# Two attention layers and a mixture of experts on one core: norm pieces of the first attention moved, its first scores issued inside the projections, two ScalarE tables fetched ahead, one low part given to VectorE

## The chip, the cores and the metric

The kernel runs on one core of a Trainium2 chip. Its time is the device time of one execution in microseconds. Each run is compared by its median; a profile is one execution recorded by the hardware profiler, and all stretches below count from the start of its span.

## What is computed

```python
x = L0_attn_x                                   # (4, 512, 256) fp32
x = x + _layernorm(attn(_layernorm(x), Wq, Wk, Wv, Wo))       # 16 heads of 16, causal
x = x + _layernorm(ffn(_layernorm(x), ...))
# ffn(h):
#   r   = rmsnorm(h, ln1_w);  16 heads of 128, causal, scale 192 ** -0.5
#   hid = h + attention(r) @ o_w.T
#   x2  = rmsnorm(hid, ln2_w)
#   w   = top 4 of softmax(x2 @ gate_w.T), normalised to sum 1     (16 experts)
#   routed = sum_e w_e * (silu(x2 @ g_e.T) * (x2 @ u_e.T)) @ w2_e.T   (176 wide)
#   shared = (silu(x2 @ sg.T) * (x2 @ su.T)) @ sh_down_w.T            (352 wide)
#   return hid + routed + shared
```

All of it is fp32; matmuls split their operands into a high part (fp32r) and a low part, and add three products.

## The kernel before

The 2048 rows (4 batches of 512) stay in SBUF as 16 tiles of 128 rows. Each engine has one instruction stream written out in order, and the streams meet through semaphores. They run through six stages.

**Projections of the first attention** (0 to 55 us). For each batch `b`, TensorE turns the normalised rows (`turn_x`), multiplies them into four banks of q and k, then into two banks of v. ScalarE copies the high parts and v out of PSUM (`ph1_hi`, `ph1_v`), VectorE forms the low parts (`ph1_lo`). Banks 0 and 1 hold the turned rows, banks 2 to 5 q and k, banks 6 and 7 v.

**First attention** (55 to 243 us): 32 steps `step1(s)`, two heads of one batch each, 8 steps to a batch. SyncE builds a "stack" for each step out of the high and low parts of q and k: seven DMAs into one of `NSTK = 4` slots (`load_stack`, line 379 for six of them, line 381 for the last), followed by one DMA that clears scratch rows in HBM (line 385). The load of step `s + 4` waits until TensorE has finished the scores of step `s`. In a step:

- TensorE computes scores of the *next* step (line 1564: the widest three blocks `S1_PARTS` early, the rest `S1_REST` later), VectorE takes the row minima of the negated scores (line 1113), TensorE turns them (line 1527, `least`), ScalarE copies them into the stack (line 837, two small copies), TensorE computes the transposed scores with that row (line 1571), ScalarE takes five exponentials (line 832), GpSimd clears the future (line 520), TensorE multiplies with the values (line 1581).
- Every second step ScalarE copies the sums out (line 850, `o_sum`), TensorE turns them, VectorE weighs them (line 1174); every fourth step TensorE turns the output and ScalarE copies it (`take_oT`, line 856).
- One batch later its rows are projected, normed and added, a piece at a time, at steps counted by `k = s % 8` and `b = s // 8 - 1`: projection at `k == 2`, `scale_u` at `k == 5` (two tiles by ScalarE, line 804; two by VectorE), the sum `x1` by GpSimd after it, GpSimd's roots at `k` 3, 4, 6, 7, and `scale_xn` at `k == 0` (two tiles by ScalarE, line 810; two by VectorE, line 1136), which waits for GpSimd's `m_rms`. The normed rows are turned at `k == 4`.

What ScalarE does in its `step1` after the stack copies, in order, in the kernel before: exponentials 0 and 1, `o_sum`, `take_oT` at `s % 8 == 1`, `scale_xn` at `k == 0`, exponentials 2 to 4, `take_oT` at `s % 8 == 5`, `scale_u` at `k == 5`. VectorE has `scale_xn` between the two groups of minima.

All engines then meet at a fence. **Second attention** (248 to 945 us): 64 heads, one after the other. **Shared expert and routing of the last batch** (945 to 1021 us): 12 pieces `s`, each with an up product on TensorE, silu by ScalarE (line 990), the product with the other half by VectorE (line 1385), its high part by ScalarE (line 994), its low part `hh_lo` by GpSimd for `s < LO_POOL = 6` (line 729) and by VectorE for the rest (line 1395), and the down product, which waits for `hh_lo`. Between them stand the norm and the routing of the last batch: squares on ScalarE (line 897), roots of them on GpSimd (12 small instructions, ahead of its first `hh_lo`), the scaled rows (lines 1223 and 904), their transposes (line 1681), copies (line 909 and 1228), logits, ranks and places on VectorE, and the sending of rows by GpSimd. **Experts** (1021 to 1195 us): 79 tiles, loaded by SyncE once all rows are sent. **End**: sums, norm, store.

ScalarE's functions come in tables. The exp table is loaded where the first exponential stands, the silu table where the first silu stands (ACT_TABLE_LOAD in the trace).

Of the kernel before, what the change touches and what calls it, by code (L numbers as in the profile page):

```python
# [17 lines left out]
ACT = mybir.ActivationFunctionType  # L18
# [3 lines left out]
P = 128  # L22
# [9 lines left out]
def sandwich_kernel(nc, x_d, qkv1_d, wo1_d, qkvo2_d, ln_w_d, gate_d, moe_d, stack_d, out_d):  # L32
# [40 lines left out]
    with ctx:  # L73
# [399 lines left out]
        def _(pool):  # L473
# [258 lines left out]
            root_of_squares(B - 1)  # L732
            for s in range(LO_POOL):
                shared_lo(s)
# [12 lines left out]
        def _(act):  # L747
# [75 lines left out]
            free = bank[FREE_BANK]  # L823

            def step1(s):
                b, k = s // (N1 // B) - 1, s % (N1 // B)

                def exp(i):
                    act.wait_ge(a1_st, 6 * s + (i + 1 if i < 2 else i + 2))
                    if i == 0 and s >= 2:  # L830
                        act.wait_ge(a1_pv, s - 1)
                    act.activation(pT1[:, s % 2, i, :], st1(s, i)[:, :], ACT.Exp).then_inc(a1_exp, 1)  # L832

                if s < N1:
                    act.wait_ge(a1_mt, s + 1)
                    for a in range(2):
                        act.activation(stk[64 * a:64 * a + 1, s % NSTK, 0, :], st1(s, 0)[64 * a:64 * a + 1, :], ACT.Copy)\
                           .then_inc(a1_m, 1)
                if b >= 0 and k == 2:
                    take_y(b, 0, free)  # L840
                if b >= 1 and k == 4:
                    take_xT(b - 1, 0, free)
                if s < N1:
                    exp(0)
                    exp(1)
                if s >= 2 and s % 2 == 0:

                    act.wait_ge(a1_pv, s)
                    act.wait_ge(a1_ot, s // 2 - 1)
                    act.activation(o1_sum[:, :], bank[O1_BANK][:, :], ACT.Copy).then_inc(a1_oe, 1)  # L850
                def take_oT():
                    g = (s - 5) // 4
                    act.wait_ge(a1_xt, g + 1)
                    if g >= 2:
                        act.wait_ge(m_y, 2 * (g // 2))
                    act.activation(oT1[:, g % 2, :], free[:, :], ACT.Copy).then_inc(a1_o, 1)

                if s >= 5 and s % 8 == 1:
                    take_oT()
                if b >= 0 and k == 2:  # L860
                    take_y(b, 1, free)
                if b >= 1 and k == 0:
                    scale_xn(b - 1)
                if b >= 1 and k == 4:
                    take_xT(b - 1, 1, free)
                if s < N1:
                    for i in range(2, 5):
                        exp(i)
                if s % 8 == 5:
                    take_oT()  # L870
                if b >= 0 and k == 5:
                    scale_u(b)

            for s in range(N1 + 2):
                step1(s)
# [100 lines left out]
            for n in range(N2 + 2):  # L976
                step2(n)
            squares(B - 1)
            def w1_half(c, gu):
# [59 lines left out]
        def _(dve):  # L1039
# [115 lines left out]
            def step1(s):  # L1155
# [32 lines left out]
                if b >= 0 and k == 5:  # L1188
                    scale_u(b)
                if b >= 1 and k == 0:  # L1190
                    scale_xn(b - 1)
                if s + 1 < N1:
# [3 lines left out]
                if b >= 1 and k == 4:  # L1196
                    take_xT(b - 1, 1, free)
                if b >= 0 and s < N1 and k == 2:
                    y_stats(b)
# [179 lines left out]
            for s in range(SHARED + 1):  # L1379
# [6 lines left out]
                if s and s % SHR == 0:  # L1386
# [3 lines left out]
                    for i in range(2):  # L1390
                        two = hs[:, TPB * b + 2 * i:TPB * b + 2 * i + 2, :].rearrange("p j d -> p (j d)")
                        dve.tensor_tensor(two, two, bank[6 + i][:, :], ALU.add).then_inc(f_acc, 1)
                if LO_POOL <= s < SHARED:
                    dve.wait_ge(f_hh, s + 1)
                    dve.tensor_tensor(hh_lo[0:rows, s % 2, :], gated[0:rows, s % 2, :], f32(hh_hi[0:rows, s % 2, :]),
                                      ALU.subtract).then_inc(f_lod, 1)
# [77 lines left out]
        def _(pe):  # L1474
# [7 lines left out]
            def turn_x(b):  # L1482
# [3 lines left out]
                for c in range(C):  # L1486
# [3 lines left out]
                    ins.then_inc(ph1_tp, 1)  # L1490

            turn_x(0)
            for b in range(B):
# [8 lines left out]
                if b + 1 < B:  # L1502
                    turn_x(b + 1)
                if b == 0:
                    pe.wait_ge(ph1_wl, 2)
                else:
                    pe.wait_ge(ph1_v, b * 2)
# [45 lines left out]
            pe.wait_ge(ph1_lo, 4 * B)  # L1553
            pe.wait_ge(ph1_v, 2 * B)
            pe.wait_ge(a1_zero, 3)
            free = bank[FREE_BANK]

            def step1(s):
# [27 lines left out]
                r = s + 1  # L1586
                if r < N1:
                    pe.wait_ge(stk_in[r % NSTK], 16 * 7 * (r // NSTK + 1))
                    for i, (a, n) in enumerate(S1_PARTS):
                        if r >= 1:  # L1590
                            pe.wait_ge(a1_max, 6 * (r - 1) + i + 4)
                        score(r, a, n).then_inc(a1_s, 1)
# [226 lines left out]
            def shared_down(s):  # L1819
                b, r = s // SHR, s % SHR  # L1820
                rows = shared_rows(r)
                if s < LO_POOL:
                    pe.wait_ge(f_lop, s + 1)
                else:
                    pe.wait_ge(f_lod, s - LO_POOL + 1)
                if b and r == 0:
# [161 lines left out]
```

## Time and profile before

| what | value |
|---|---|
| median of 3 runs | 1240.77 us (1239.87 to 1243.07) |
| the profiled execution | 1242.91 us, its span 1241.2 us |
| TensorE busy in matmuls | 1178.2 us, 95% of the span |
| VectorE, ScalarE, GpSimd busy | 861.5, 794.0, 577.1 us |
| first attention, 80 to 100 us | TensorE 19.05 of 20 us, ScalarE 16.25, VectorE 16.75 |
| second attention, 500 to 600 us | TensorE 100.0 of 100 us |
| mean granted clock of TensorE | 0.986 of full speed |

The busy shares are averages over stages with different limits. The chain of waits follows the work that ended last back to what released it; the timeline gives each engine's instructions with their start, their time and, in brackets, how long the engine had been idle and what ended that.

### The profile page before, as it was taken

The page shows a single profiled execution, that of the slowest core. Times are in us where ns is not written, and L with a number is a line of the kernel's source. Part 1 is how long each engine was busy: PE and PEld are TensorE (multiplying, and loading weights), DVE is VectorE, ACT ScalarE, POOL GpSimd, SP SyncE. Part 2 cuts the span into 40 slices and gives each one's busy share as a digit, 9 for nine tenths or more (in the row PEclk, how much of TensorE's full clock was granted, in tenths as well). Part 3 has the DMA queues.
Part 4 walks back from the last instruction along what each step waited for, and adds up shares of the span by engine and source line. Part 5 has one row for each costly group of instructions (what it writes and reads, how often), then busy time and mean ns, then how long its engine had stood idle before and what let it go on. Part 6 is the DMA issues. An engine that isn't in the chain of part 4 may idle for free.

```text
span 1241.2 us, 25176 instructions
## 1 busy us (share of the span) xinstructions
PE 1178.2 (95%) x7996; PEld 1007.7 (81%) x7996; DVE 861.5 (69%) x2662; ACT 794.0 (64%) x1971; POOL 577.1 (47%) x845
## 2 busy tenths in 40 slices
PE   6899999889999999999999999999998889999986
PEld 5756555579999998999989999989997769999962
DVE  5677887677667666886667876777865855555535
ACT  3387777767768776677676777776776534444422
POOL 3053645545333444537443366433363346666650
PEclk9989999999999999999999999999999989999998
DMA  8955555175733112122212122121214247777766
GB/s 266 283 160 174 172 167 152 51 213 152 213 109 95 54 55 87 48 70 83 86 35 69 35 68 105 35 68 35 69 61 113 68 124 122 117 118 119 117 113 218
DMA packets 111780, 139.59 MB, mean 112 GB/s; under 512 B 11364, under 2 KB 94820, under 8 KB 111524
## 3 DMA queue, kind: packets, MB, share of 16 engines
q1 hardware_dynamic: 97204, 119.10, 31.6%
q0 software_dynamic: 14448, 18.88, 9.4%
q8 instruction: 69, 1.13, 0.4%
q14 instruction: 59, 0.48, 0.1%
HBM read 63.36 MB, written 61.87 MB: 101 GB/s over the span
## 4 chain that ended last, share of the span: by engine, by line
PE 70%; DVE 12%; ACT 8%; issue 4%; POOL 3%; DMA 2%; SPq 1%; POOLq 0%; ACTq 0%; DVEq 0%
PE bank L1478 49%; PE bank L1887 5%; PE bank L1710 5%; DVE bank L1113 3%; PE bank L1527 3%; PE bank L1581 2%; ACT p L953 2%; PE bank L1564 2%; DVE hs L1336 2%; ACT pT L832 2%; DVE pT L1323 1%; PE bank L1866 1%; PE bank L1897 1%; PE bank L1571 1%; DVE qk L1212 1%
## 5 line engine op out<-in xcount | busy, mean ns | idle before, releaser
L1113 DVE CUSTOM_DVE_ANT_0 bank<-bank,mask 128x512 f32<-128x512 f32 (+3 forms) x512 | 235.2, 523 | 35.8 <-PE bank L1564 23.1
L944 ACT ACTIVATE p<-bank,stat 128x512 f32<-128x512 f32 (+3 forms) x256 | 131.7, 528 | 132.2 <-DVE stat L1113 132.2
L533 POOL CAST w_hl<-raw_qkv 128x512 fp32r<-128x512 f32 x96 | 58.8, 613 | 312.3 <-DMA raw_qkv<-in_qkvo 162.6
L1478 PE MATMUL bank<-xT,w_hl 128*128 128x512 f32 x768 | 189.2, 395 | 0.0
L1478 PEld LDWEIGHTS bank<-xT,w_hl 128*128 128x128 f32 x768 | 144.1, 188 | 34.1
L742 POOL DMA_INDIRECT sum_rows<-mid,goal x79 | 122.9, 1555 | 70.7 <-DVE mid L1442 69.2
L1478 PE MATMUL bank<-pT,v 128*128 128x128 f32 (+3 forms) x768 | 137.1, 327 | 0.0
L953 ACT ACTIVATE p<-p,stat 128x512 f32<-128x512 f32 (+3 forms) x256 | 123.1, 553 | 14.7 <-DVE stat L1339 14.7
L1478 PE MATMUL bank<-qk 128*128 128x512 f32 (+3 forms) x768 | 129.4, 317 | 3.2 <-DVE pT L1323 2.4
L1478 PEld LDWEIGHTS bank<-qk 128*128 128x128 f32 x768 | 119.3, 189 | 12.1 <-DVE v L1212 2.6
L534 POOL TENSOR_TENSOR w_hl<-raw_qkv,w_hl 128x512 fp32r<-128x512 f32 x96 | 124.2, 1294 | 7.8
L1361 DVE TENSOR_TENSOR o<-bank,o 128x512 fp32r<-128x512 f32 x64 | 44.2, 690 | 109.4 <-ACT o L960 109.4
L1478 PEld LDWEIGHTS bank<-pT,v 128*128 128x128 f32 x768 | 109.7, 190 | 2.9
L1478 PE MATMUL bank<-wo_hl,o 128*128 128x256 f32 x768 | 107.2, 289 | 2.8 <-DVE o L1361 1.4
L1323 DVE TENSOR_TENSOR pT<-bank,pT 128x128 fp32r<-128x128 f32 (+3 forms) x256 | 107.2, 481 | 0.0
L1478 PEld LDWEIGHTS bank<-w_hl,xT 128*128 128x128 f32 x768 | 98.8, 188 | 9.5 <-issue 4.3
L1478 PE MATMUL bank<-w_hl,xT 128*128 128x256 f32 x768 | 101.5, 280 | 1.9 <-DVE xT L1228 1.9
L832 ACT ACTIVATE pT<-bank 128x512 f32<-128x512 f32 x160 | 85.2, 602 | 24.8 <-PE bank L1571 23.2
L1478 PEld LDWEIGHTS bank<-wo_hl,o 128*128 128x128 f32 x768 | 95.6, 190 | 4.3 <-issue 2.5
L1478 PE MATMUL bank<-w_hi,sh_hi 128*128 x316 | 97.2, 349 | 0.5 <-issue 0.4
L1212 DVE SCALAR_TENSOR_TENSOR qk<-bank,qk 128x512 fp32r<-128x512 f32 x128 | 82.4, 683 | 21.7 <-ACT qk L886 21.4
L936 ACT ACTIVATE pT<-bank 128x128 fp32r<-128x128 f32 (+3 forms) x256 | 91.1, 454 | 0.0
(232 smaller groups left out, 2404.0 us busy)
## 6 DMA issues: line engine op xcount, KB each, us to landing
raw_qkv<-in_qkvo SPq DMA_DIRECT2D x32, 768.0 KB, 5.7
xs_rows<-blank SPq DMA_DIRECT2D x32, 520.0 KB, 3.3
xs_rows<-blank SPq DMA_DIRECT2D x5, 2730.0 KB, 14.3
xrow<-xs_rows SPq DMA_DIRECT2D x79, 130.0 KB, 2.5
raw_o<-in_qkvo SPq DMA_DIRECT2D x32, 256.0 KB, 3.7
sum_rows<-blank SPq DMA_DIRECT2D x3, 2176.0 KB, 8.5
stk<-xT SPq DMA_DIRECT2D x96, 64.0 KB
stk<-k_hl SPq DMA_DIRECT2D x96, 64.0 KB
```

Of the source, the lines that this page charges most:

```text
L534: pool.tensor_tensor(lo, raw, f32(hi), ALU.subtract).then_inc(done, 1)
L742: pool.indirect_dma_start(sum_d[i % NSUM], bass.IndirectOffsetOnAxis(goal[:, i % NY:i % NY + 1], 0), yt[:, i % NY, :], None, compute_op=AL ...
L832: act.activation(pT1[:, s % 2, i, :], st1(s, i)[:, :], ACT.Exp).then_inc(a1_exp, 1)
L936: act.activation(pT2[:, HI, QOFF[kj]:QOFF[kj + 1]], bank[t][:, 0:TB - P * kj], ACT.Copy).then_inc(b_pth, 1)
L944: act.activation(p2[:, n % 2, POFF[qi]:POFF[qi + 1]], s2(t), ACT.Exp, scale=-1.0, bias=stat2[:, 0, n % 2, t:t + 1], accum_out=stat2[:, 1, ...
L953: act.activation(pt, pt, ACT.Copy, scale=stat2[:, 2, n % 2, t:t + 1]).then_inc(b_norm, 1)
L1113: return dve.tensor_tensor_reduce(scores, scores, mask[:, TB - scores.shape[1]:], scale=-1.0, scalar=-2.0 * MASKED, op0=ALU.add, op1=ALU.m ...
L1212: dve.scalar_tensor_tensor(lo, qkv_bank(n, i)[:, :], SCALE2 if i == 0 else 1.0, f32(hi), ALU.mult, ALU.subtract).then_inc(b_lo, 1)
L1323: dve.tensor_tensor(pT2[:, LO, QOFF[kj]:QOFF[kj + 1]], bank[t][:, 0:TB - P * kj], f32(pT2[:, HI, QOFF[kj]:QOFF[kj + 1]]), ALU.subtract).th ...
L1478: ins = pe.matmul(out, a, b, start=start and i == 0, stop=stop and i == len(pairs) - 1, **kw)
L1710: ins = pe.transpose(bank[t][:, P * (qi - kj):P * (qi - kj + 1)], p2[:, (n - 1) % 2, POFF[qi] + P * kj:POFF[qi] + P * (kj + 1)], ident[:, :])
L1887: ins = pe.matmul(bank[6 + i % 2][:, 0:D], ht[:, i % 2, P * h:P * (h + 1)], w2r[:, ds(expert[i], 1), h, :].rearrange("p a n -> p (a n)"), ...
```

## The change

1. The wait for all value copies (`ph1_v`, 8) goes from TensorE's start of the first attention, and the three widest score blocks of step 0 (`first_scores`) are issued in the last batch's projections, after q and k and ahead of v.
2. ScalarE's `take_oT` of `s % 8 == 5` stands in the next step, right after its stack copies.
3. ScalarE's `scale_u` stands between exponentials 1 and 2 of the same step, no longer at its end.
4. `scale_xn` of ScalarE and VectorE stands at the end of the step with `k == 1`, no longer in the middle of the one with `k == 0` (only for the last batch it stays at `k == 0`, after the last step).
5. A one-element exponential ahead of `step1(0)` and a one-element silu ahead of the last `squares` load the two tables there.
6. The low part of the first shared piece is VectorE's; GpSimd has pieces 1 to 5.

```diff
@@ gpsimd
-            for s in range(LO_POOL):
+            for s in range(1, LO_POOL):
                 shared_lo(s)
@@ scalar, step1
+                if s >= 6 and s % 8 == 6:
+                    take_oT((s - 6) // 4)
                 if b >= 0 and k == 2:
                     take_y(b, 0, free)
...
                     exp(0)
                     exp(1)
+                if b >= 0 and k == 5:
+                    scale_u(b)
                 if s >= 2 and s % 2 == 0:
...
                 if s >= 5 and s % 8 == 1:
-                    take_oT()
+                    take_oT((s - 5) // 4)
                 if b >= 0 and k == 2:
                     take_y(b, 1, free)
-                if b >= 1 and k == 0:
-                    scale_xn(b - 1)
...
                     for i in range(2, 5):
                         exp(i)
-                if s % 8 == 5:
-                    take_oT()
-                if b >= 0 and k == 5:
-                    scale_u(b)
-
+                if b >= 1 and k == (1 if s < N1 else 0):
+                    scale_xn(b - 1)
+
+            act.activation(sm[:, 10, 0:1], ident[:, 0:1], ACT.Exp)
             for s in range(N1 + 2):
                 step1(s)
...
             for n in range(N2 + 2):
                 step2(n)
+            act.activation(sm[:, 9, 0:1], ident[:, 0:1], ACT.Silu)
             squares(B - 1)
@@ vector
-                if b >= 1 and k == 0:
-                    scale_xn(b - 1)
...
+                if b >= 1 and k == (1 if s < N1 else 0):
+                    scale_xn(b - 1)
...
-                if LO_POOL <= s < SHARED:
+                if s == 0 or LO_POOL <= s < SHARED:
                     dve.wait_ge(f_hh, s + 1)
@@ tensor
+            def first_scores():
+                pe.wait_ge(stk_in[0], 16 * 7)
+                for a, n in S1_PARTS:
+                    if n == 2:
+                        pe.wait_ge(ph1_lo, 4 * (B - 1) + 1)
+                    rows = slice(64 * a, 64 * a + 64)
+                    pe.matmul(s1(a, n), stk[rows, 0, 0, P * (n - 1):P * n], stk[rows, 0, 1, 0:P * n],
+                              start=True, stop=True).then_inc(a1_s, 1)
...
                 if b + 1 < B:
                     turn_x(b + 1)
+                else:
+                    first_scores()
...
-            pe.wait_ge(ph1_v, 2 * B)
...
-                if s < LO_POOL:
-                    pe.wait_ge(f_lop, s + 1)
+                if 1 <= s < LO_POOL:
+                    pe.wait_ge(f_lop, s)
                 else:
-                    pe.wait_ge(f_lod, s - LO_POOL + 1)
+                    pe.wait_ge(f_lod, s - LO_POOL + 2 if s else 1)
```

The order of instructions at three places, before and now.

TensorE, end of the projections and step 0 of the first attention (`bank<-stk` are scores; the row of 24 with 128x256 is v of the last batch). Before:

```order
L1478 MATMUL bank<-xT,qkv_hl 128x512 x24
L1478 MATMUL bank<-qkv_hl,xT 128x256 x24
L1564 MATMUL bank<-stk 128x512 x2
L1564 MATMUL bank<-stk 128x256
L1564 MATMUL bank<-stk 128x384 x2
```

Now:

```order
L1479 MATMUL bank<-xT,qkv_hl 128x512 x24
L1500 MATMUL bank<-stk 128x512 x2
L1500 MATMUL bank<-stk 128x256
L1479 MATMUL bank<-qkv_hl,xT 128x256 x24
L1576 MATMUL bank<-stk 128x384 x2
```

Three score matmuls have moved ahead of the 24 of v.

ScalarE, steps 16 and 17 of the first attention (`stk<-bank` are the stack copies at the start of a step, `pT<-bank` exponentials, `xn_mid` is `scale_xn`). Before:

```order
L837 ACTIVATE stk<-bank 1x512 x2
L832 ACTIVATE pT<-bank 128x512 x2
L850 ACTIVATE o_sum<-bank 128x512
L810 ACTIVATE xn_mid<-x_sb,midst 128x256 x2
L832 ACTIVATE pT<-bank 128x512 x3
L837 ACTIVATE stk<-bank 1x512 x2
L832 ACTIVATE pT<-bank 128x512 x2
L856 ACTIVATE oT<-bank 128x512
L832 ACTIVATE pT<-bank 128x512 x3
L837 ACTIVATE stk<-bank 1x512 x2
```

Now:

```order
L843 ACTIVATE stk<-bank 1x512 x2
L838 ACTIVATE pT<-bank 128x512 x2
L860 ACTIVATE o_sum<-bank 128x512
L838 ACTIVATE pT<-bank 128x512 x3
L843 ACTIVATE stk<-bank 1x512 x2
L838 ACTIVATE pT<-bank 128x512 x2
L829 ACTIVATE oT<-bank 128x512
L838 ACTIVATE pT<-bank 128x512 x3
L810 ACTIVATE xn_mid<-x_sb,midst 128x256 x2
L843 ACTIVATE stk<-bank 1x512 x2
```

`scale_xn` has moved from the middle of step 16 to the end of step 17, ahead of the stack copies of step 18.

VectorE, start of the shared expert. Before:

```order
L1336 TENSOR_TENSOR hs<-hs,bank 128x512 x2
L1385 TENSOR_TENSOR gated<-gated,bank 128x512
L1223 TENSOR_SCALAR mid<-hs,midst 128x256 x2
L1385 TENSOR_TENSOR gated<-gated,bank 128x512
L1228 SCALAR_TENSOR_TENSOR xT<-bank,ln_w,xT 128x512 x2
```

Now:

```order
L1337 TENSOR_TENSOR hs<-hs,bank 128x512 x2
L1386 TENSOR_TENSOR gated<-gated,bank 128x512
L1396 TENSOR_TENSOR hh_lo<-gated,hh_hi 128x512
L1224 TENSOR_SCALAR mid<-hs,midst 128x256 x2
L1386 TENSOR_TENSOR gated<-gated,bank 128x512
```

One low part stands ahead of VectorE's half of the last norm.

## Rows read from the trace of the kernel before

**Rows 1.** Busy time and share of the span, TensorE (page, part 1).

```profile
PE 1178.2 (95%) x7996; PEld 1007.7 (81%) x7996; DVE 861.5 (69%) x2662; ACT 794.0 (64%) x1971; POOL 577.1 (47%) x845
```

**Rows 2.** Timeline, start of the first attention: start, us, engine, line, operation [idle before].

```profile
51.23 3.03 PE L1478 MATMUL bank<-qkv_hl,xT 128*128 128x256 f32 x24
...
55.16 0.58 PE L1564 MATMUL bank<-stk 64*128 64x512 f32 x3 [0.91 <-issue]
55.81 0.70 DVE L1113 CUSTOM_DVE_ANT_0 bank<-bank,mask 128x512 f32<-128x512 f32 x1 [2.97 <-PE bank L1564]
...
57.28 0.77 PE L1564 MATMUL bank<-stk 64*128 64x384 f32 x4 [0.21 <-DVE least L1113]
...
62.77 1.28 ACT L832 ACT_TABLE_LOAD   x1
```

**Rows 3.** Stretches: busy (count) of PE, PEld, DVE, ACT, POOL, clock, DMA share, GB/s.

```profile
58.80:69.00 10.20, 9.36 (x37) 5.52 (x39) 6.47 (x28) 6.29 (x10) 3.05 (x6) 0.53 0.66 210
...
150.80:154.20 3.40, 3.40 (x20) 1.71 (x19) 1.76 (x8) 2.05 (x4) 2.53 (x6) 0.61 0.37 99
```

**Rows 4.** Timeline, ScalarE in step 13.

```profile
131.63 1.09 ACT L832 ACTIVATE pT<-bank 128x512 f32<-128x512 f32 x2 [0.61 <-PE bank L1571]
133.44 1.57 ACT L832 ACTIVATE pT<-bank 128x512 f32<-128x512 f32 x3 [0.72 <-PE bank L1571]
134.89 0.62 ACT L856 ACTIVATE oT<-bank 128x512 f32<-128x512 f32 x1
135.37 1.11 ACT L804 ACTIVATE mid<-mid,midst 128x256 f32<-128x256 f32 x2
```

**Rows 5.** Timeline, VectorE and ScalarE in steps 16, 17 and 18.

```profile
148.18 0.74 DVE L1136 TENSOR_SCALAR xn_mid<-x_sb,midst 128x256 f32<-128x256 f32 x2 [1.68 <-POOL midst L573]
...
149.12 1.09 ACT L810 ACTIVATE xn_mid<-x_sb,midst 128x256 f32<-128x256 f32 x2
...
152.10 1.20 ACT L837 ACTIVATE stk<-bank 1x512 fp32r<-1x512 f32 x2 [0.43 <-PE bank L1527]
...
155.28 1.09 ACT L832 ACTIVATE pT<-bank 128x512 f32<-128x512 f32 x2 [1.97 <-PE bank L1571]
...
161.10 0.60 ACT L797 ACTIVATE mid<-bank 128x512 f32<-128x512 f32 x1 [1.22 <-PE bank L1478]
```

**Rows 6.** Timeline and chain: SyncE's stack loads, and TensorE's score weights that wait for them.

```profile
76.68 2.12 SPq L379 DMA_DIRECT2D stk<-xT  x3
...
103.97 1.56 DMA stk<-stk
...
152.35 0.51 SPq L381 DMA_DIRECT2D stk<-stk  x1
...
156.95 0.30 PEld L1564 LDWEIGHTS bank<-stk 64*128 64x128 f32 x3
...
158.69 2.13 SPq L379 DMA_DIRECT2D stk<-xT  x3
...
204.64 0.30 PEld L1564 LDWEIGHTS bank<-stk 64*128 64x128 f32 x3
```

**Rows 7.** Timeline, shared expert and routing of the last batch.

```profile
948.34 1.28 ACT L990 ACT_TABLE_LOAD   x1
...
949.64 0.60 ACT L990 ACTIVATE gated<-bank 128x512 f32<-128x512 f32 x1
...
952.19 1.27 POOL L729 TENSOR_TENSOR hh_lo<-gated,hh_hi 128x512 fp32r<-128x512 f32 x1
...
953.52 0.47 PE L1478 MATMUL bank<-sh_hi,hh_hi 128*128 128x256 f32 x1 [2.19 <-POOL hh_lo L729]
...
957.23 1.27 ACT L909 ACTIVATE xT<-bank,ln_w 128x512 fp32r<-128x512 f32 x2 [0.41 <-PE bank L1681]
...
959.28 3.15 DVE L1376 SCALAR_TENSOR_TENSOR w_lo<-w_raw,ln_w,w_hi 128x2816 fp32r<-128x2816 f32 x1
...
963.56 0.29 DVE L1236 TENSOR_REDUCE lg<-bank 128x64 f32<-128x128 f32 x1 [0.54 <-PE bank L1478]
```

More of the change, by code:

```diff
@@ L823, in _, with take_oT @@
             free = bank[FREE_BANK]
+            def take_oT(g):
+                act.wait_ge(a1_xt, g + 1)
+                if g >= 2:
+                    act.wait_ge(m_y, 2 * (g // 2))
+                act.activation(oT1[:, g % 2, :], free[:, :], ACT.Copy).then_inc(a1_o, 1)
             def step1(s):
@@ L850, in step1 @@
                     act.activation(o1_sum[:, :], bank[O1_BANK][:, :], ACT.Copy).then_inc(a1_oe, 1)
[L851 to L856, printed above, removed]
                 if s >= 5 and s % 8 == 1:
-                    take_oT()
+                    take_oT((s - 5) // 4)
                 if b >= 0 and k == 2:
                     take_y(b, 1, free)
-                if b >= 1 and k == 0:
-                    scale_xn(b - 1)
                 if b >= 1 and k == 4:
@@ L1586, in step1 @@
                 r = s + 1
-                if r < N1:
+                if 1 <= r < N1:
                     pe.wait_ge(stk_in[r % NSTK], 16 * 7 * (r // NSTK + 1))
                     for i, (a, n) in enumerate(S1_PARTS):
-                        if r >= 1:
-                            pe.wait_ge(a1_max, 6 * (r - 1) + i + 4)
+                        pe.wait_ge(a1_max, 6 * (r - 1) + i + 4)
                         score(r, a, n).then_inc(a1_s, 1)
```

## The prediction

> **What bounds the kernel now.** The page's busy times come first: TensorE is at 95% [rows 1], so a change that gives it no less work can only take away time in which it waits or runs at its low clock. The timeline then says where that time lies, and in which waits. At the start of the first attention TensorE waits 0.91 us with nothing of its own to do and VectorE waits 2.97 us for the first scores [rows 2]; the stretches show that TensorE then has 1.2 GHz (granted clock 0.53 of full) over most of 58.8 to 69.0 us [rows 3]. Inside the first attention a step is a ring through TensorE, VectorE and ScalarE. ScalarE closes it: in step 13 it does its two extra pieces (0.62 and 1.11 us) with no wait ahead of them [rows 4], and in step 16 it does `scale_xn` for 1.09 us and then makes TensorE late [rows 5]. The third stretch is the shared expert: TensorE waits 2.19 us for the first low part of GpSimd [rows 7]. The second attention and the experts are TensorE's own work; neither is touched, so what is gained ahead of them moves them as a whole.
>
> **The start.** The three score matmuls cost 0.58 us and now stand ahead of v [rows 2]. v (51.23, 3.03 us long) ends 0.58 later, at 54.84. VectorE had been idle since 52.84 and takes its first three minima 2.97 earlier. So TensorE, once v is done, can issue the second set of scores at once: the row at 57.28 comes at about 55.0, 2.3 us earlier [rows 2]. v's copies on ScalarE end 0.6 later, and only GpSimd's first copy of v needs them, ten us ahead of its use; that costs nothing. The exp table, 1.28 us on the path at 62.77, goes to a time at which ScalarE waits; the transposed scores are then the limit, about half of the load later, so I count 0.7. The turn of the minima falls before the clock falls and takes some 0.4 less. Together 3.4; I take 3.3, since SyncE's next loads start in a stretch in which the DMA rings are busy (share 0.66 over 58.8 to 69.0) [rows 3]. From below the bound is 2.3, the scores alone. From above it is 4.9: if the clock never falls, at most half of the 10.2 us at low clock can come back, and since VectorE and ScalarE hold TensorE for much of that I allow 1.5 of it.
>
> The load itself is weighed against the Trainium skill. In this trace both table loads last 1.28 us and the next function follows within 0.02 us [rows 7]. The Trainium skill ("ScalarE: Activation LUTs", What ACT_TABLE_LOAD costs) puts a switch at 1.28 us for the load and some 1.38 us more for a drain. By that rule the two moved loads would give up to 2.8 us more, an estimate from the page; the trace shows no drain, and the sum goes by the trace.
>
> **Steps 13, 21 and 29** (`k == 5`). `take_oT` and `scale_u` take about 0.5 and 1.0 from start to start [rows 4], at the end of the step, directly ahead of the next stack copies. Now `scale_u` stands after the first two exponentials, where ScalarE waited 0.72 for TensorE, and `take_oT` after the stack copies, where it waits 0.61 for the transposed scores [rows 4]. Both waits are covers: 0.5 goes wholly into the second, 0.7 of 1.0 into the first. 1.5 less 0.3 left over is 1.2, and as the last exponentials come 0.3 later for TensorE I take 1.1 for each. GpSimd's sum `x1` starts earlier too and holds up nobody new.
>
> **Steps 16 to 18, and 24 to 26.** In step 16 `scale_xn` costs ScalarE 1.09, after which its stack copy still waits 0.43 [rows 5]: 1.5 together. VectorE waits 1.68 in it for GpSimd's roots, with the minima of the next step queued behind; TensorE runs dry, its clock is 0.61 from 150.8 to 154.2 [rows 3], and the exponentials of step 17 wait 1.97 in place of 0.61 [rows 4, 5]: 1.4 more. So 2.9 goes. What is moved to the end of step 17 (1.1 on ScalarE, 0.7 on VectorE) stands ahead of the copies of step 18. There TensorE does the 2 us of output projection before it asks for them, and ScalarE waited 1.22 behind its copies [rows 5], so 1.1 fits. Without that cover it would cost 1.1. The roots are ready a step earlier, so nobody waits for GpSimd.
>
> **The cap.** A batch of steps gains 1.1 + 2.9 = 4.0 on the compute engines. SyncE's queue does not get faster: load 6 starts at 76.68 and load 21 at 158.69, back to back, 5.47 us for each [rows 6]. The scores of step 19 (156.95) need the load whose last DMA is issued at 152.35 and lands 1.56 later, at 153.9 [rows 6]; they can come 3.0 earlier and no more. So the first batch gives 3.0. From 156.95 to 204.64, eight steps, the loads allow 47.7 less 8 x 5.47 = 3.9 [rows 6], so the second gives 3.9. The third has only step 29, 1.1. First attention: 3.0 + 3.9 + 1.1 = 8.0. Its bounds are 4.3 (rival 1) and 9.1 (uncapped).
>
> **The shared expert.** The silu table leaves the path, so the first silu (949.64) comes at 948.35, 1.3 earlier [rows 7], and product and high part with it. GpSimd reached the low part only behind its roots, at 952.19, and took 1.27; VectorE, idle there, needs about 0.7 and is done at 951.1. TensorE ends its up products at 951.3 and goes on at once, 2.2 earlier than 953.52 [rows 7]. The roots end at 952.2 as before and are not moved by this, so less arrives at the routing: ScalarE's weight piece, which stands before its half of the norm, ends 1.2 earlier, and its copies of the turned rows (957.23) come at about 955.8. VectorE's 3.15 us piece moves from 959.28 to 957.9 and holds it until 961.0; with the next product the logits start at 961.8 in place of 963.56, where TensorE had been the later one [rows 7]. 1.8 then. VectorE is nearly full up to the sending of the rows, GpSimd's sending, SyncE's tile loads and the experts follow in a chain, and all carry the 1.8. Bounds: 0.7 (only half of the 1.3 passes the handovers) and 2.2 (TensorE's whole wait).
>
> **The sum.** 3.3 + 8.0 + 1.8 = 13.1 us. Against the profiled execution (1242.91 us, span 1241.2) that is 1229.8. That execution lies 2.1 above the median of the runs, 1240.77; against the median it is **1227.7 us**.
>
> **The rivals.**
>
> 1. *The moved `scale_xn` costs in its new place what it did in the old one.* If TensorE asks for the stack copies of step 18 earlier than the projection lets me think, 1.1 of ScalarE shows up again, and with a late TensorE the low clock of 150.8 us stays. Then a batch gives 1.1 + 0.5, the attention 1.6 + 1.6 + 1.1 = 4.3; with 2.8 at the start and 1.5 at the end it is 8.6, so 1232.2. For it: the low clock of 150.8 [rows 3] came with waits that were each under 2 us [rows 5], so a short one may be enough. Against it: the 1.22 that ScalarE waited behind those copies [rows 5].
> 2. *More than the sum.* The clock stays up at the start (4.9), SyncE's loads space closer than 5.47 (9.1), and the shared part gives 2.2: 16.2, so 1224.6. For it: the waits at the start that let TensorE go slow are mostly gone. Against it: the queue was saturated for 82 us [rows 6].
> 3. *The time is the same.* SyncE is the bound over the whole attention: loads that start earlier stand in a full ring behind the scratch clears and end when they did, so that start and steps give back all but the third batch's 1.1. With 1.8 at the end it is 1237.9. Against it: in the later batches the loads come four and more us ahead of their use.
> 4. *Slower: the low clock spreads.* The place is the first attention, where moved pieces leave other, shorter holes in TensorE's work and the clock falls in more steps. The price is 1.4 a step [rows 4, 5]. It decides from the point where more than nine steps have it, for then 13 us are given back; at fourteen steps it is 1247. Against it: the two low places shown [rows 3] lie behind waits that the change shortens.
>
> That the change doesn't do what it says is hardly a case: the order of instructions shows the three scores ahead of v, one table load in each new place and no second one behind the squares. Stack slot 0 is loaded long before 51 us.
>
> **How the numbers follow.** Forecast 0.64, rival 1 0.20, rival 2 0.09, rival 3 0.04, rival 4 0.03. The range takes the forecast with its bounds, rival 1 with 1.5 above it, and most of rival 2: 1224 to 1234. What a measurement of this kernel can tell from no change is 0.3%, or 3.7 us: below 1237.0 is faster. The forecast and rivals 1 and 2 are below it: 0.93. Rival 3 is within: 0.04. Rival 4 is above 1244.5: 0.03.
>
> **What the profile of the changed kernel would show.** The first `bank<-stk` row would stand at about 51.2 us and the first exponential near 60.6 in place of 64. The steps with `k == 0` would be as short as their neighbours (4.7 us), the ones with `k == 5` about 5.4, and VectorE's `xn_mid` would wait for nobody. ScalarE's copies of step 18 would be followed by a shorter wait than 1.22. First attention would end about 11 us earlier. The first down product of the shared expert would follow its up product with no wait, and the logits' first VectorE row would lie 1.8 closer to the last head's end. It would be wrong if stack copies of steps 18 or 26 were waited for by TensorE, if SyncE's loads took more than 5.5 us each, or if the clock were low in places where it is full now.

## The result, and the profile of the changed kernel

| | before | changed |
|---|---|---|
| median of 4 runs, same series | 1241.92 us (1239.87 to 1244.19) | 1232.24 us (1230.65 to 1232.67) |
| the profiled execution, its span | 1242.91, 1241.2 us | 1231.81, 1230.1 us |
| TensorE busy, granted clock | 1178.2 us, 0.986 | 1172.6 us, 0.989 |

The ratio is 0.9915, 95% interval [0.9898, 0.9932]: 9.7 us faster by the medians, 11.1 by the two profiled executions. The forecast was 1227.7, 13.1 faster. All shares below are of those 11.1 us. I cut both traces at the same events; each row of the table starts where the row above it ends:

| from the timelines | before | changed | difference | forecast |
|---|---|---|---|---|
| start to the end of the last q and k products | 51.23 | 51.13 | -0.10 | 0 |
| from there to the first exponential | 12.84 | 9.30 | -3.54 | -3.3 |
| to the stack copy of step 31 | 172.31 | 164.29 | -8.02 | -8.0 |
| to the first shared up product | 709.31 | 709.26 | -0.05 | 0 |
| to the turning of the sixth expert tile | 79.07 | 79.19 | +0.12 | -1.8 |
| to the last accumulation, start to start | 174.84 | 174.84 | 0 | 0 |
| to the end | 41.51 | 42.00 | +0.49 | 0 |

In the sum, the first attention gave what it was to give; between these two traces the shared part gave nothing.

**The start.** Timeline of the changed kernel, TensorE and ScalarE (columns as in [rows 2]).

```profile
51.13 0.61 PE L1500 MATMUL bank<-stk 64*128 64x512 f32 x3
51.67 3.14 PE L1479 MATMUL bank<-qkv_hl,xT 128*128 128x256 f32 x24
54.74 0.68 PE L1576 MATMUL bank<-stk 64*128 64x384 f32 x5
...
55.52 1.28 ACT L873 ACT_TABLE_LOAD   x1
...
60.43 1.58 ACT L838 ACTIVATE pT<-bank 128x512 f32<-128x512 f32 x3 [0.88 <-PE bank L1583]
```

Stretches of it (columns as in [rows 3]).

```profile
56.00:66.00 10.00, 9.45 (x43) 5.52 (x43) 7.07 (x31) 6.01 (x11) 3.68 (x7) 0.66 0.82 262
66.00:70.00 4.00, 4.00 (x48) 2.65 (x45) 3.58 (x17) 3.73 (x7) 2.18 (x5) 1.00 0.65 202
```

The second set of scores stands at 54.74 (forecast 55.0, before 57.28 [rows 2]), the table load in idle time. The low clock is still there, but ends before 66, where it lasted to 69 [rows 3].

**Steps 13, and 16 to 18.** ScalarE of the changed kernel.

```profile
125.47 1.18 ACT L843 ACTIVATE stk<-bank 1x512 fp32r<-1x512 f32 x2
127.27 1.09 ACT L838 ACTIVATE pT<-bank 128x512 f32<-128x512 f32 x2 [0.61 <-PE bank L1583]
128.24 1.09 ACT L804 ACTIVATE mid<-mid,midst 128x256 f32<-128x256 f32 x2
129.22 1.08 ACT L838 ACTIVATE pT<-bank 128x512 f32<-128x512 f32 x2
...
142.79 1.08 ACT L838 ACTIVATE pT<-bank 128x512 f32<-128x512 f32 x2 [0.59 <-PE bank L1583]
143.76 0.61 ACT L860 ACTIVATE o_sum<-bank 128x512 f32<-128x512 f32 x1
...
147.74 1.08 ACT L838 ACTIVATE pT<-bank 128x512 f32<-128x512 f32 x2 [0.68 <-PE bank L1583]
...
151.16 1.11 ACT L810 ACTIVATE xn_mid<-x_sb,midst 128x256 f32<-128x256 f32 x2
152.14 1.18 ACT L843 ACTIVATE stk<-bank 1x512 fp32r<-1x512 f32 x2
```

A step is counted from its stack copies on ScalarE to those of the next. `scale_u` fills the former 0.72 wait [rows 4]; step 13 takes 5.52 us in place of 6.51. The exponentials of step 17 wait 0.68, not 1.97 [rows 5]. `scale_xn` now stands at 151.16, directly ahead of the copies of step 18.

**The cap, and what is late next.** Weights of TensorE and the queue of SyncE at step 19, then step 15 on TensorE and ScalarE.

```profile
148.56 0.51 SPq L381 DMA_DIRECT2D stk<-stk  x1
...
150.14 0.29 PEld L1576 LDWEIGHTS bank<-stk 64*128 64x128 f32 x3 [0.61 <-DMA stk<-stk]
...
136.63 1.16 PE L1576 MATMUL bank<-stk 64*128 64x384 f32 x5
...
137.96 1.81 ACT L838 ACTIVATE pT<-bank 128x512 f32<-128x512 f32 x3 [1.12 <-PE bank L1583]
...
133.87 1.40 DVE L1144 BATCH_NORM_STATS2 mid<-x_sb 128x6 f32<-128x256 f32 x4
```

The scores of step 19 come 1.58 us after the load's last DMA is issued; before they came 4.60 after it (156.95 and 152.35, [rows 6]). In this trace the forecast cap is reached: steps 11 to 18 take 43.74 us, 46.59 before: 2.85 gained, 3.0 forecast. Steps 19 to 26 gain 3.44 (forecast 3.9), steps 27 to 30 gain 0.99 (1.1). That is 7.28 of the 8.02; the other 0.73 came in the steps before 11, where the sum had nothing (step 5, with a `take_oT` of its own, took 5.05 in place of 5.53). That the total came out at 8.0 to the tenth is in part luck. One cost was not forecast: steps 15 and 23 take 5.35 us each, 4.88 before. VectorE's statistics (L1144) now end after TensorE has turned the minima, so the minima of the next step start 0.71 us behind that turn (0.06 ahead of it before), TensorE's five scores at 136.63 take 1.16 us (0.67 before), and ScalarE waits 1.12 us.

**The shared expert.** Timelines of VectorE, GpSimd and TensorE in the changed kernel.

```profile
938.51 0.69 DVE L1396 TENSOR_TENSOR hh_lo<-gated,hh_hi 128x512 fp32r<-128x512 f32 x1 [0.70 <-ACT hh_hi L995]
...
949.34 0.28 DVE L1237 TENSOR_REDUCE lg<-bank 128x64 f32<-128x128 f32 x1
...
950.05 3.14 DVE L1377 SCALAR_TENSOR_TENSOR w_lo<-w_raw,ln_w,w_hi 128x2816 fp32r<-128x2816 f32 x1
...
950.16 4.16 POOL L729 TENSOR_TENSOR hh_lo<-gated,hh_hi 96x512 fp32r<-96x512 f32 x1 [5.04 <-ACT hh_hi L995]
...
954.37 0.39 PE L1479 MATMUL bank<-sh_hi,hh_hi 96*128 96x256 f32 x1 [2.56 <-POOL hh_lo L729]
...
990.73 3.15 DVE L1377 SCALAR_TENSOR_TENSOR w_lo<-w_raw,ln_w,w_hi 128x2816 fp32r<-128x2816 f32 x1
...
991.08 3.64 POOL L680 DMA_INDIRECT xs_rows<-xrow,idx  x1 [0.31 <-issue]
995.03 0.97 POOL L680 DMA_INDIRECT xs_rows<-xrow,idx  x1 [0.30 <-issue]
```

At first all went as forecast or better: the first low part at 938.51, the first down product with no wait ahead of it, VectorE's first row of the logits 15.36 us after the first up product in place of 17.87, 2.5 closer. That is more than the 1.8 of the forecast, and TensorE's clock has part in it, which the forecast left out. Some 8 us after the first up product, a stretch of before and one of the changed kernel:

```profile
953.69:955.69 2.00, 2.00 (x10) 2.00 (x11) 0.41 (x2) 1.74 (x4) 0.00 (x0) 0.50 1.15 285
```

```profile
941.98:943.98 2.00, 1.95 (x13) 1.71 (x14) 0.69 (x1) 1.25 (x3) 0.15 (x1) 1.00 1.12 297
```

Behind the 2.19 us wait for the first low part [rows 7] TensorE had 1.2 GHz (0.50); without that wait it keeps 2.4 GHz (1.00). Then VectorE's `w_lo` (low parts of the expert weights; two operands in SBUF, 3.14 us) starts 0.11 us ahead of GpSimd's low part of piece 2, which takes 4.16 us where others take 1.29; TensorE waits 2.56 us for it. At the end another `w_lo` starts 0.35 us ahead of GpSimd's 15th send (one indirect DMA of rows for the experts), which takes 3.64 in place of 0.97.

The same places before:

```profile
963.76 1.29 POOL L729 TENSOR_TENSOR hh_lo<-gated,hh_hi 96x512 fp32r<-96x512 f32 x1 [5.58 <-ACT hh_hi L994]
...
964.14 0.99 DVE L1239 TENSOR_TENSOR lg<-lg,col 128x64 f32<-128x64 f32 x1
965.05 3.14 DVE L1376 SCALAR_TENSOR_TENSOR w_lo<-w_raw,ln_w,w_hi 128x2816 fp32r<-128x2816 f32 x1
...
1003.57 0.99 POOL L680 DMA_INDIRECT xs_rows<-xrow,idx  x1 [0.31 <-issue]
1004.86 2.76 POOL L680 DMA_INDIRECT xs_rows<-xrow,idx  x1 [0.30 <-issue]
...
1003.63 3.15 DVE L1376 SCALAR_TENSOR_TENSOR w_lo<-w_raw,ln_w,w_hi 128x2816 fp32r<-128x2816 f32 x1
```

There GpSimd came first at piece 2, and VectorE's small subtraction paid (0.99, 0.23 in the changed kernel); and `w_lo` started 0.06 us behind a send, so that this send passed and only the last was held. The 16 sends took 23.01 us from the first to the last, 24.27 in the changed kernel. The first send is 1.17 closer to the first up product (37.75, before 38.92), and the longer sends take that back. The Trainium skill ("SBUF — State Buffer", Who interferes with whom) has the rule: a VectorE instruction with two SBUF inputs and a GpSimd one that reads SBUF exclude each other, and whichever issues first holds the other for its whole length. The rows agree in what they show of the low part: 0.11 us behind an instruction of 3.14 us it is 2.87 us longer.

**Theory:** start and first attention are worth what was forecast; the shared part's gain is real up to the logits and is lost to such collisions, first at piece 2, then at the sends. **Rival:** the single edits are worth other amounts (the moved `scale_xn` costs in its new place, SyncE decides), and the sum agrees by chance. A third cause could stand behind the sends: they may be held whatever the shared edits do.

### The profile page after: what moved, and what is told of

It reads as the page before. It is cut to its first block, busy times and chain, and to the rows that moved or that the text cites. A ratio compares the mean times of both kernels' runs of the same rounds, so it can differ in the third digit from the quotient of the medians.

```text
span 1230.1 us, 25177 instructions
## 1 busy us (share of the span) xinstructions
PE 1172.6 (95%) x7996; PEld 1004.9 (82%) x7996; DVE 859.6 (70%) x2663; ACT 794.0 (65%) x1973; POOL 580.0 (47%) x844
## 4 chain that ended last, share of the span: by engine, by line
PE 69%; DVE 13%; ACT 8%; issue 4%; POOL 2%; DMA 2%; SPq 1%; ACTq 0%; POOLq 0%
PE bank L1479 49%; PE bank L1898 5%; PE bank L1721 5%; DVE bank L1114 3%; PE bank L1540 2%; PE bank L1576 2%; PE bank L1593 2%; ACT p L953 2%; DVE hs L1337 2%; DVE pT L1324 1%; PE bank L1877 1%; POOL xs_rows L680 1%; PE bank L1908 1%; PE bank L1583 1%; DVE qk L1213 1%
```

## The experiments

Each kernel is the changed one with one edit (u_shared, u_start and v_late2 have two, u_ot undoes two moves, v_best joins four). Stretches from each one's trace: A from the end of the last q and k products to the first exponential; B from there to the stack copy of step 31; C from the first shared up product to the first send of the last batch; D from the same up product to the sixth expert tile.

| kernel | median, ratio to before [95%] | A | B | C | D |
|---|---|---|---|---|---|
| before | | 12.84 | 172.31 | 38.92 | 79.07 |
| changed | 1232.24, 0.9915 [0.9898, 0.9932] | 9.30 | 164.29 | 37.75 | 79.19 |
| after_again | 1230.05, 0.9920 [0.9905, 0.9935] | 9.31 | 164.56 | 37.76 | 79.23 |
| u_shared | 1231.63, 0.9916 [0.9902, 0.9929] | 9.30 | 163.49 | 38.39 | 79.85 |
| u_start | 1233.39, 0.9931 [0.9917, 0.9944] | 12.84 | 164.39 | 38.97 | 80.48 |
| u_exp | 1231.76, 0.9932 [0.9917, 0.9948] | 9.98 | 164.22 | 40.48 | 81.01 |
| u_xn | 1232.51, 0.9935 [0.9922, 0.9949] | 9.30 | 167.20 | 37.73 | 79.12 |
| u_ot | 1233.24, 0.9944 [0.9929, 0.9959] | 9.54 | 166.77 | 37.74 | 79.22 |
| u_silu | 1233.39, 0.9941 [0.9928, 0.9955] | 9.31 | 164.52 | 40.35 | 82.01 |
| v_clear | 1233.38, 0.9919 [0.9905, 0.9934] | 9.30 | 163.37 | 37.73 | 79.16 |
| v_lo2 | 1230.14, 0.9900 [0.9885, 0.9916] | 9.30 | 164.42 | 36.31 | 79.12 |
| v_late2 | 1228.13, 0.9889 [0.9874, 0.9904] | 9.30 | 163.48 | 37.74 | 77.97 |
| v_pieces | 1230.45, 0.9909 [0.9894, 0.9924] | 9.30 | 164.83 | 37.74 | 79.05 |
| v_best | 1226.60, 0.9887 [0.9872, 0.9903] | 9.30 | 163.45 | 36.33 | 76.53 |

Medians alone don't tell edits of 1 us apart; the stretches repeat within 0.03 us where nothing disturbs them, and B, with the low clock at its start and the loads in it, lies between 163.5 and 164.8 in the kernels that have the first attention of the changed one. The end behind the last accumulation, which no edit touches, took 39.33 to 42.03 us; so the last column matters more than the span.

**after_again** is the changed kernel unaltered.

> The changed kernel unaltered, to be compared within this series. Theory: 9.7 us faster than before as measured, 0.9922 of its time. In its trace the value products' start to the first exponential, the first attention (164.3 us from the first exponential to the last stack copy) and the 4.16 us low part of piece 2 repeat; the end behind the last accumulation, which no edit touches, varies between 39.4 and 42.0.

B, C and D repeat within 0.3 us, and the low part of piece 2 takes 4.16 us again.

**u_start** has the start undone, **u_exp** its table load alone.

```diff
-                else:
-                    first_scores()
...
-            act.activation(sm[:, 10, 0:1], ident[:, 0:1], ACT.Exp)
```

> The changed kernel with its start undone: the first scores behind the value products and the exp table loaded at the first exponential. Theory (the stream of stack loads starts with the first scores and so moves as a whole): 3.6 us slower, 1235.9, with steps 16 to 18 as short as in the changed kernel. Rival (SyncE's loads set steps 16 to 19 whatever the start): less than 2 us slower.

> The changed kernel without the exponential that loads the table ahead of the first attention. The prediction's term: the table was worth 0.7 us, half of its 1.28, as the transposed scores are the next limit. Theory: the first exponential comes 1.3 later, step 1 starts 0.7 later, 1232.9 against 1232.2. Rival: VectorE or TensorE still set step 1 and nothing is lost.

In u_start A is 12.84 again, to the hundredth, and B (164.39) and steps 16 to 18 (18.36, 18.35) are as short as in the changed kernel: the start is worth 3.54 us and the stream of loads moves with it, so the rival's mechanism is not there. Its number is: by the ratios of the medians u_start is only 1.4 to 2.0 us slower than the changed kernel, not 3.6. The intervals are wider than the difference, so the 3.54 rests on the traces. In u_exp the table alone is 0.68 of the 3.54 (forecast 0.7).

**u_xn** has item 4 undone (both `scale_xn` at `k == 0`), **u_ot** items 2 and 3.

```diff
-                if b >= 1 and k == (1 if s < N1 else 0):
+                if b >= 1 and k == 0:
                     scale_xn(b - 1)
```

```diff
-                if s >= 6 and s % 8 == 6:
-                    take_oT((s - 6) // 4)
...
+                if s % 8 == 5:
+                    take_oT((s - 5) // 4)
+                if b >= 0 and k == 5:
+                    scale_u(b)
```

> The changed kernel with scale_xn of ScalarE and VectorE back in the middle of the step with k = 0. Theory: steps 16 and 17 and steps 24 and 25 are as long as before (6.2 and 6.6 us), the low clock at step 16 is back: 4.3 us slower by what the two batches gained beyond steps 13 and 21 (1.85 and 2.45), 1236.5. Rival (its new place costs as much as the old one): less than 1.5 us slower.

> The changed kernel with take_oT and scale_u back at the end of their step. Theory (loads cap the first batch, so that what step 13 loses is made up by step 19): steps 13, 21, 29 are each 1.0 longer and steps 15 and 23 each 0.5 shorter, but the first batch loses nothing, the second 0.5, the third 1.0: 1.5 to 2 us slower, 1233.7 to 1234.2. Rival (the pieces add up, no cap): 3.0 for the three steps and 0.5 for step 5, 3.5 slower.

u_xn loses 2.9 us in B, not 4.3. Its steps 16 to 18 take 18.94 us, its steps 24 to 26 20.45 (20.70 before). The difference lies beside TensorE's clock, here in u_xn around the start of each of them:

```profile
144.00:150.00 6.00, 5.65 (x58) 3.68 (x58) 5.43 (x26) 4.89 (x10) 2.96 (x7) 1.00 0.66 188
...
188.00:194.00 6.00, 5.50 (x44) 3.02 (x34) 4.53 (x21) 4.77 (x10) 3.03 (x8) 0.79 0.57 168
```

Against the 17.75 of steps without a wait for a load the piece costs 1.2 us where the clock stays full and 2.7 where it falls to 1.2 GHz for part of the time (0.79). The forecast's 2.9 was the second case. In u_ot steps 13, 21 and 29 are 1.0 longer each and 15 and 23 are 4.87 again; steps 11 to 18 take 43.65 (43.74 with the edit), so against the changed kernel's trace the first batch loses nothing, the second 0.5, the third 1.0, as expected under the cap. But no scores wait for a load in u_ot, and against the traces of the changed attention in which none do (43.15, see v_clear) the first batch loses 0.5 too. The steps before 11 and A lose another 1.4, more than the 0.5 that I had for step 5; 0.9 of it is step 1, which the edit doesn't touch and which takes between 4.6 and 5.9 us from trace to trace.

**v_clear** clears half as many scratch rows behind each load.

```diff
-        CLEAR_FIRST, CLEAR_STEP, CLEAR_LATE = 24, 4, 5
+        CLEAR_FIRST, CLEAR_STEP, CLEAR_LATE = 24, 2, 5
```

> The changed kernel with 2 in place of 4 row blocks of scratch cleared after each stack load, the rest after the first attention. Theory (the loads of steps 17 to 19 and 10, 11 cap the first batch because the clears share the DMA rings): loads come closer than 5.4 us, no scores wait for a load, first attention ends 0.5 to 1.2 us earlier: 1231.3. Rival (SyncE's issue time or VectorE is the next bound): within 0.3 us.

No scores wait for a load. Steps 16, 17, 18 take 4.67, 6.20, 6.89: 17.76, 2.92 less than before, the uncapped term. The loads do come closer: the closest follow each other in 4.70 us, 5.05 with the full clears. But that the cap goes by this is not shown. With the full clears steps 16 to 18 take 17.76 to 17.80 too in u_exp, v_lo2, v_late2 and u_shared, and steps 11 to 18 take 43.15 to 43.17 (43.13 here), a gain of 3.43 on before and more than the 3.0 of the cap; the scores of steps 18 and 19 wait there for no load, or for 0.3 us. From load 6 to load 21 their loads follow each other in 5.34 to 5.42 us, in the changed kernel's trace in 5.45. So the cap holds in five traces of the changed attention with full clears (the changed kernel, after_again, u_start, u_silu, v_pieces) and not in four. B, 163.37, is 0.9 less than in the changed kernel and only 0.1 less than in u_shared and v_late2. No gain is seen in the median, as the rival had it. In this trace the second attention takes 0.8 more, with a low clock some 15 us after its start; u_shared and u_exp, which clear as before, and v_best had that too.

**u_shared** has items 5 (silu) and 6 undone, **u_silu** the silu alone.

```diff
-            act.activation(sm[:, 9, 0:1], ident[:, 0:1], ACT.Silu)
...
-                if s == 0 or LO_POOL <= s < SHARED:
+                if LO_POOL <= s < SHARED:
```

> The changed kernel with its shared-expert part undone: no silu ahead of the last squares, first low part back on GpSimd. Theory (the shared part's gain is lost again to collisions of VectorE's and GpSimd's instructions): the time is that of the changed kernel within 0.5 us, 1231.7 to 1232.8; GpSimd's low part of piece 2 is back at some 1.3 us, where it took 4.16, and only the last of the sends is held. Rival (the 1.8 us of the prediction are there and something else in the change costs them): 1234.0.

> The changed kernel without the silu that loads the table ahead of the last squares. Theory: first silu, product, high and low part and the first down product each 1.3 to 1.4 us later, TensorE waits some 0.9 us there, sends start 0.4 to 1.3 later, and the low part of piece 2 meets w_lo or not by the 0.1 us between them; the experts start within 0.7 us of the changed kernel. The prediction's term would be 1.3 us slower.

u_shared's time is that of the changed kernel, as the theory has it. Its low part of piece 2 takes 1.28: that collision stands in all ten traces with the shared edits (or item 6 of them) and the low part on GpSimd, and in neither without them. But its 15th send, 0.18 us behind a `w_lo`, takes 3.81:

```profile
991.49 3.15 DVE L1376 SCALAR_TENSOR_TENSOR w_lo<-w_raw,ln_w,w_hi 128x2816 fp32r<-128x2816 f32 x1
991.67 3.81 POOL L680 DMA_INDIRECT xs_rows<-xrow,idx  x1 [0.30 <-issue]
```

So the longer hold of the sends is not made by the shared edits. My expectation that only the last would be held was wrong. The code of its shared part is that of before, and gives D 79.07 in one trace and 79.85 in the other, sends 23.01 and 24.26 in all. Measured against u_shared, the shared edits gave 0.66 (79.85 to 79.19); measured against before, nothing. With one trace of each, neither is firm to better than 0.8. u_silu is 2.8 later in D, twice the 1.4 of its silu. The rest stands behind the same wait of 2.56 us, where the clock is low again. Here three traces with that wait, changed, u_exp and u_start:

```profile
954.00:962.00 8.00, 7.63 (x45) 6.59 (x46) 5.76 (x27) 3.30 (x5) 2.86 (x3) 1.00 0.00 1
```

```profile
955.00:963.00 8.00, 8.00 (x30) 7.01 (x31) 3.45 (x17) 1.94 (x3) 1.27 (x1) 0.58 0.00 0
```

```profile
958.00:966.00 8.00, 8.00 (x40) 6.81 (x40) 5.10 (x27) 2.51 (x3) 1.84 (x2) 0.79 0.00 0
```

Of ten traces with the collision at piece 2, three have a low clock behind it: C is 1.2 longer in u_start, 2.7 in u_exp, and 2.6 in u_silu, 1.4 of it the silu's own. The changed kernel's own trace is one of the lucky seven: there was luck in its 79.19.

**v_lo2** gives VectorE the low part of piece 2, ahead of `w_lo`.

```diff
                 if s == 2:
                     logits_less_max(B - 1, bank[4])
+                    dve.wait_ge(f_hh, s + 1)
+                    dve.tensor_tensor(hh_lo[0:rows, s % 2, :], gated[0:rows, s % 2, :], f32(hh_hi[0:rows, s % 2, :]),
+                                      ALU.subtract).then_inc(f_lod, 1)
                     w1_rest(0, 1)
```

> The changed kernel with the low part of piece 2 on VectorE too, ahead of the w_lo instruction of 3.1 us with which GpSimd's low part collided. Theory (GpSimd's low part took 4.16 in place of 1.29 us because it ran beside w_lo, and TensorE waited 2.56 for it): that wait goes, the fifth silu and the sends come 1.0 to 1.3 earlier: 1231.1. Rival (the sends hang on logits and ranks, not on the low part): within 0.3 us of the changed kernel.

```profile
949.61 0.69 DVE L1407 TENSOR_TENSOR hh_lo<-gated,hh_hi 96x512 fp32r<-96x512 f32 x1
950.22 3.14 DVE L1377 SCALAR_TENSOR_TENSOR w_lo<-w_raw,ln_w,w_hi 128x2816 fp32r<-128x2816 f32 x1
...
956.04 0.39 PE L1482 MATMUL bank<-sh_hi,hh_hi 128*128 128x256 f32 x1 [0.55 <-POOL hh_lo L729]
```

A stretch of the same trace, at the start of the experts:

```profile
1009.00:1014.00 5.00, 4.85 (x20) 4.35 (x21) 1.63 (x5) 1.23 (x4) 0.89 (x2) 0.66 0.54 118
```

The 2.56 wait is gone (what is left is 0.55, for piece 3) and the sends start 1.44 earlier; the rival falls. Against before the first send is now 2.6 closer to the first up product: what the logits had gained arrives. D doesn't show it, since this trace has a second low clock there (0.66; 1.00 in the same stretch of the changed kernel).

**v_late2** puts both last `w_lo` behind the last low part and the last shared sum behind the first two tiles; **v_pieces** cuts the third `w_lo` in four.

```diff
-                if s >= SHARED - 2 and s < SHARED:
-                    w1_rest(1, s - SHARED + 2)
+                if s == SHARED - 1:
+                    w1_rest(1, 0)
+                    w1_rest(1, 1)
```

```diff
+                if SHARED - 4 <= s < SHARED:
+                    w1_rest(1, 0, s - SHARED + 4, 4)
+                if s == SHARED - 1:
+                    w1_rest(1, 1)
```

> The changed kernel with both of the last w_lo instructions behind the last low part, after GpSimd's sends, and the last sum of the shared expert behind the first two tiles of the experts. Theory (a send waits while w_lo runs): no send is longer than 1.4 us, the last rows land 2.7 us earlier, and the experts start 1.2 us earlier, then held by w_lo: 1231.0. Rival (sends are slow for another reason, DMA queues): the 15th send is still 3.6 us, and the time is the same or longer.

> The changed kernel with the third w_lo instruction cut into four of 0.8 us, one in each of the last four pieces. Theory (a send waits for the rest of a VectorE instruction with two SBUF inputs, so at most 0.8 us at a time): the longest send falls from 3.64 to about 1.8, the held time in all from 2.7 to 1 to 1.6 us, and the experts start 1 us earlier: 1231.2. Rival (the hold depends on the sum of VectorE's time, not on one instruction's): the sends end as in the changed kernel.

The last sends of v_late2, then the longest one of v_pieces with its VectorE row:

```profile
986.68 1.36 POOL L680 DMA_INDIRECT xs_rows<-xrow,idx  x1 [0.28 <-POOL xrow L678]
988.35 0.97 POOL L680 DMA_INDIRECT xs_rows<-xrow,idx  x1 [0.30 <-issue]
989.63 0.97 POOL L680 DMA_INDIRECT xs_rows<-xrow,idx  x1 [0.30 <-issue]
990.90 0.97 POOL L680 DMA_INDIRECT xs_rows<-xrow,idx  x1 [0.30 <-issue]
```

```profile
984.80 1.87 POOL L680 DMA_INDIRECT xs_rows<-xrow,idx  x1 [0.30 <-issue]
...
984.87 0.94 DVE L1378 SCALAR_TENSOR_TENSOR w_lo<-w_raw,ln_w,w_hi 128x704 fp32r<-128x704 f32 x1
```

With `w_lo` away no send is held by it; all sends take 21.58 us (24.27), and the sixth tile is turned 1.2 us earlier as expected (the first 2.3). The kernel has two edits at once, and the 1.2 is not divided between them. With pieces a send is held for one piece at a time (1.87), and all sends take 23.20 us: 1.1 is given back. D gains only 0.1, not the 1 us expected; its trace has the low clock at the experts' start that v_lo2's has.

**v_best** joins v_lo2, v_clear and v_late2, with half of the third `w_lo` left one piece earlier.

> The changed kernel with four edits: low part of piece 2 on VectorE, the third w_lo instruction in two halves (one in the last piece but one, one behind the last low part), the last shared sum behind the first two expert tiles, half as much scratch cleared per stack load. Theory (costs add up, each at its own place): first attention 163.4 us from the first exponential to the last stack copy (0.9 less), sends start 1.4 earlier behind the last head, experts start 3.8 us earlier behind it, 1.2 by w_lo out of the sends, 1.4 by piece 2, 1.2 by the half that starts earlier: 4.7 less than the changed kernel in this series, 1227.5. Rival (TensorE's work or the rows' landing is the next bound): not more than the 2.5 that piece 2 and the sends gave apart.

It is the fastest: 0.9887, against 0.9920 for the changed kernel in its series, 3.5 us less by the medians (4.7 expected); the two intervals do not meet. B is 1.1 and D 2.7 less than after_again's. The 1.1 of B is for a good part that no scores wait for a load, which happens with the full clears too. Of the forecast 3.8 in D the half gave next to nothing: it held a send for 1.4, and TensorE still waited for rows (2.52 us, 2.96 in the changed kernel). That is the rival: little more than the 2.5 that piece 2 and the sends gave apart.

## Why the prediction was right, and where it was not

The measured 1232.24 lies in the stated range, 1224 to 1234, and on the side that was forecast. The mechanism came out for the start and the first attention; of the forecast 13.1 us, 9.7 came by the medians.

- **Start, 3.3:** right. 3.54, with 0.68 for the table and the second scores 0.3 from where they were put.
- **Steps 13, 21, 29, 1.1 each:** right (1.0 each). The two waits covered the pieces. Step 5 gave 0.48 in the same way and was left out of the sum.
- **Steps 16 to 18, 2.9:** right as a sum (2.92 where no scores wait for a load). Undone alone, `scale_xn` is worth 1.2 or 2.7, by the clock.
- **The cap, 3.0 and 3.9:** near in size in this trace, 2.85 and 3.44, but not the fixed bound that it was put as. The scores of steps 18 and 19 do wait for their loads here; in four traces of the same attention they don't, the first batch gives 3.43, and the loads follow each other closer than 5.47. The missing 0.5 of the second batch is step 23, where VectorE is late next (step 15 costs the first batch the same). I had not looked at VectorE there. The total, 8.02 for 8.0, is right by the 0.73 that the steps before 11 gave unforecast.
- **Rival 1** (`scale_xn` costs in its new place): refuted. In v_clear the stack copies of step 18 do start 1.0 later behind their turn, and the exponentials 3.90 us behind the turn, exactly as before: the projection covers it.
- **"All carry the 1.8":** this is the step that failed. Up to the logits the gain was 2.5, more than forecast, with a low clock that went. It did not arrive: I took VectorE and GpSimd as two queues whose instructions keep their lengths when they shift. The shift of VectorE against GpSimd turned who comes first at piece 2 (a hold of 2.9 us and TensorE's wait of 2.56), which left 1.17 at the first send. The sends then took 1.26 more (longest hold 2.7 us in place of 1.8). That is the same mechanism, but not the edit's doing: u_shared has it with the old code. Against before nothing was left, +0.12 in place of -1.8.
- **The level:** between the profiled executions the forecast is 2.0 off (1229.8, 1231.8): 1.9 by the shared term and 0.5 by the end, less 0.4 by the start and small ones. The other 2.5 of the 4.5 us lies in the step to the median: I took off 2.1 since the profile of before stood that far above its median, and the changed kernel's stands 0.4 below.

Still open: what makes the clock fall behind one and the same wait in three traces of ten, and at the start of the second attention in some; what spaces the stack loads differently from trace to trace; and what decides whether a `w_lo` meets the sends in the unaltered shared code. No run was made for these.

## What to carry to other kernels

When a change shifts two engines against each other, look in the trace for pairs that may exclude each other (here VectorE with two SBUF operands and GpSimd) and ask who will come first afterwards; a lead of 0.1 us decided over 2.9 us. Put long instructions of such a pair where the other engine has nothing due. And compare traces by stretches cut at the same events: the edits of 1 us that medians cannot tell repeat there to some hundredths.

## What the runs showed that I had not expected

- GpSimd's indirect DMA sends are held by VectorE instructions with two SBUF inputs: 3.64 us beside `w_lo` (3.15), 1.36 beside a low part (0.68), while GpSimd's copies beside `hs<-hs,bank`, which has one input in PSUM, keep their 0.20. The same section of the Trainium skill infers that a tensor_tensor does not do this to descriptor generation. Here the row of 1.36 speaks against it, unless the send is held while it reads its indices from SBUF; no run here tells the two apart.
- TensorE's clock is a second, uneven price of a wait: behind the 2.56 us wait it fell in three traces of ten, for 1.2 to 2.7 us more.
